# A four-layer graph network on one core: the node stage in three parts per block, five gather passes with single PSUM banks

## The chip, the core and the metric

The kernel runs on one core of a Trainium2 chip. The core has five engines with an instruction queue each: TensorE (PE, with its weight loads as PEld), VectorE (DVE), ScalarE (ACT), GpSimd (POOL) and SyncE (SP, which issues plain DMAs). Each engine works through its own queue in order; engines meet only through semaphores that an instruction waits for or raises. The metric is the device time of one launch in microseconds, median of several runs; lower is better.

## The reference

Inputs are x of 100000 nodes by 128 features, 25000 edges (src, dst, sorted by dst), edge features of 160, edge weights, and the weights of four layers. Everything is float32.

```python
x = layernorm(x + L0(x)); x = layernorm(x + L1(x)); x = layernorm(x + L2(x)); x = layernorm(x + L3(x))
# L0: x + softplus-MLP(segment_sum(edge_attr, dst))
# L1: (x @ Wself.T + mean-like(segment_sum(w * x[src], dst)) @ Wneigh.T + biases) / 2
# L2: relu(x @ w_s + segment_sum((x @ w_n)[src], dst))
# L3: two Chebyshev convolutions, 128 -> 256 (relu) -> 128, each of three terms,
#     lap(h) = segment_sum(w[:, None] * h[src], dst), terms x, lap(x), 2 * lap(lap(x)) - x
```

Only nodes that are the end of an edge differ from the plain per-node chain "add, normalize, multiply, normalize, ...". The kernel uses that: it does the plain chain for all 100000 nodes, and the edges' corrections for 25000 slots.

## The kernel before

The edges are cut into 196 tiles of 128, four tiles to a quad, 49 quads (`QUADS`). Nodes are cut into 196 blocks of 512 (`BLOCKS`). The program is fully unrolled; the order of the instructions is written out by hand in "turns": turn c does the first step of item c, a later step of item c-1, and so on. A `Signal` is a semaphore that counts the turns of one producer; `s.wait(engine, pass, g, back=n)` waits until the producer has done item g-n. Between stages all five engines meet (`enter`, `leave`).

The stages in order are: a setup that builds index tables; `tgt0` and `src0` (edge rows through the first layers); `nodes`; then the gather passes `L1`, `L2`, `T1`, `T2`, `LH`; and `LU`, which scatters the finished rows over the output. The change touches `nodes` and the five passes from L1 to LH; tgt0, src0 and LU keep their order.

**The node stage** (`row_pass("nodes", BLOCKS)`) takes one block per turn. In the names of the profile: GpSimd adds a constant (y0, L599); TensorE turns y0 (L1383) and ScalarE copies it out of PSUM (yTa, L1137); TensorE multiplies it (p1, L1527); VectorE takes the moments of y0 (bn, L969, and mv, L974) and makes y1 from p1 (L1023); TensorE turns y1, ScalarE copies it (yTb), TensorE multiplies (p2, L1533); VectorE makes u2 (L1037) and its moments; GpSimd makes x3 from u2, four instructions (L622), and x3b, which is x3 plus the row gb2 (L609); TensorE turns x3, ScalarE copies it (yTc), TensorE makes h (L1547, two matrix products into two banks), ScalarE its relu (hT, L1273), TensorE p3 (L1540); VectorE adds x3b (y3, L1043), takes the moments; ScalarE makes the square root (sd3, L1142) and, after VectorE's reciprocal (rs3, L991) and offset (off3, L999), the output rows (outb, L1307), which SP stores. GpSimd also issues two small look-ups per block (L647). Turn c does y0, p1 and y1 of block c, p2 and u2 of block c-1, x3 of c-2, h of c-3, p3 and y3 of c-4, and sd3 and the output of c-5.

**A gather pass** (`edge_pass`) takes one quad per turn. GpSimd gathers four times 128 rows (L563); ScalarE scales them with the edge weight (L1154, not in L2); TensorE turns them into `bank(g.b)`, one of two PSUM banks (L1401); VectorE runs the scan along the sorted edges that sums each segment (L853); TensorE multiplies the sums (L1426 to L1485), and VectorE and ScalarE finish the row, which SP stores as the next pass's table. In T2 TensorE makes a first product (L1453), VectorE adds a loaded array (L903), ScalarE takes the relu (L1236), TensorE multiplies it (L1480) and turns it (L1485), and ScalarE copies both out (L1210, L1213). GpSimd gathers quad g after the sums of quad g-3:

```python
run_turns(QUADS, 0, lambda g: gather(p, g, table_, index, rows, g.r, width, rows_in, [(summed, 3)]))
```

A layout's `bank(n)` is PSUM bank n as four pieces of 128 columns; `g.b` alternates between two buffers, `g.r` runs round four.

Of the kernel before, what the change touches and what calls it, by code (L numbers as in the profile page):

```python
# [9 lines left out]
ALU = mybir.AluOpType  # L25
ACT = mybir.ActivationFunctionType

P = 128
# [3 lines left out]
HID = 256  # L32
# [10 lines left out]
RING = 4  # L43
assert TILES == 4 * QUADS and QUADS % 2 == 1 and BLOCKS % 2 == 0

# [64 lines left out]
def gnn_kernel(nc, x, src, dst, attr, ew, W1, b1, W2, b2, Wself, bself, Wneigh, bneigh, ws, wn, G1, gb1, G2, gb2, out):  # L110
    ctx = ExitStack()
    with ctx:
# [54 lines left out]
        xin, y0, y1, u2, x3, x3b, outb = (sb(n, [P, 2, 4, P]) for n in ("xin", "y0", "y1", "u2", "x3", "x3b", "outb"))  # L167
# [10 lines left out]
        lk = sb("lk", [P, 2, 4])  # L178
# [4 lines left out]
        pre_in = (y0, x3b, xin, outb)  # L183
# [9 lines left out]
        SELF, NEIGH = (5, 3), (7, 6)  # L193
        HALVES = ((6, 7), (3, 5))
        FIRST = (5, 7)

# [11 lines left out]
        LATE = {"tgt0": 3, "L1": 1, "L2": 1, "T1": 1, "T2": 1, "LH": 1, "LU": 1}  # L208
# [5 lines left out]
        def transfer(name, at_once=2, **n):  # L214
# [6 lines left out]
        x_in = transfer("x_in", nodes=1)  # L221
        xe_in = transfer("xe_in", RING, L1=1, L2=1, T1=1, LH=1, LU=1)
        pre_arrived = transfer("pre_arrived", RING, T2=1)
# [4 lines left out]
        look_in = transfer("look_in", nodes=2)  # L228
        out_st = transfer("out_st", tgt0=1, src0=1, nodes=1)
        oe_st = transfer("oe_st", RING, L1=1, L2=1, T1=1, T2=1, LH=1)  # L230
        more_st = transfer("more_st", src0=1, T1=1, T2=1, LH=1)
# [5 lines left out]
        x3b_made = signal("x3b_made", "nodes")  # L237
# [3 lines left out]
        y3_made, bn3, mv3, rs3, off3_made, looked_up = (  # L241
            signal(n, "nodes") for n in ("y3_made", "bn3", "mv3", "rs3", "off3_made", "looked_up"))
# [11 lines left out]
        out_made = signal("out_made", "tgt0 nodes L1 L2 LH LU")  # L254
# [4 lines left out]
        sd1, h_kept = signal("sd1", "src0"), signal("h_kept", "src0 T2")  # L259
        sd3 = signal("sd3", "nodes")  # L260
        hidden = signal("hidden", {"nodes": 2, "T2": 1})
# [7 lines left out]
        y0_turned, p1_made, y1_turned, p2_made, x3_turned, h_made = (  # L269
            signal(n, "src0 nodes") for n in ("y0_turned", "p1_made", "y1_turned", "p2_made", "x3_turned", "h_made"))  # L270
# [6 lines left out]
        h_turned = signal("h_turned", "T2")  # L277
# [44 lines left out]
        spb, = (yTc[:, n, :] for n in range(1))  # L322
# [3 lines left out]
        LOADS, EDGE_LOADS = 15, 12  # L326
        COUNTED = [c for c in range(TILES) if c % 3 == 0]
        PUT = [c for c in range(TILES) if c % 3 != 0]
        V_COLS, V_WEIGHTS, V_BTC, V_TABLE = 1, 2, 3, 4
        T_TURNED, T_FOLDED, T_A1, T_COUNTED = 1, 2, 3, 4  # L330
# [5 lines left out]
        def _(sp):  # L336
# [6 lines left out]
            with nc.allow_non_contiguous_dma("edge lists with an edge per partition; columns of biases"):  # L343
# [15 lines left out]
                for t, s in ((b1_col, b1), (bs_col, bself), (bn_col, bneigh)):  # L359
                    load(t[:, :], s.rearrange("(p a) -> p a", a=1))  # L360
# [16 lines left out]

            def edge_pass(p, state=None, store=None):
                def state_load(g):
                    if state is None or not g.inside(QUADS):  # L380
                        return
                    if p in ("L1", "T1"):
                        turned.wait(sp, p, g, back=RING)
                    if p == "L2":
                        step.wait(sp, p, g, back=RING)
                    if p == "LH":
                        out_made.wait(sp, p, g, back=RING)
                    if p == "LU":
                        step.wait(sp, p, g, back=RING, k=2)
                    sp.dma_start(xe[:, g.r], quad_of(state, g)).then_inc(xe_in.of(g), 16)  # L390

                def more_load(g):
                    if not g.inside(QUADS):
                        return
                    if p == "T2":
                        pre_added.wait(sp, p, g, back=RING)
                        sp.dma_start(flat(pre_in[g.r]), one(h_pre, g)).then_inc(pre_arrived.of(g), 16)
                    if p == "LU":
                        step.wait(sp, p, g, back=2, k=3)
                        sp.dma_start(gb_in[:, g.b], quad_of(state3, g)).then_inc(x3_in.of(g), 16)  # L400

                def turn(g):
                    state_load(g.less(-3))
                    more_load(g.less(-3 if p == "T2" else -1))
                    g = g.less(LATE[p])
                    if not g.inside(QUADS):
                        return
                    if p == "T1":
                        lap_kept.wait(sp, p, g)
                    elif p == "T2":  # L410
                        near_kept.wait(sp, p, g)
                    elif p != "LU":
                        out_made.wait(sp, p, g)
                    if store is not None:
                        sp.dma_start(quad_of(store, g), oe[:, g.r]).then_inc(oe_st.of(g), 16)
                    if p == "T1":
                        pre_kept.wait(sp, p, g)
                        sp.dma_start(one(h_pre, g), hb[:, g.b].rearrange("p k d -> p (k d)")).then_inc(more_st.of(g), 16)
                    if p == "T2":
                        h_kept.wait(sp, p, g)  # L420
                        sp.dma_start(quad_of(state_h, g), hb[:, g.b]).then_inc(more_st.of(g), 16)
                    if p == "LH":
                        u_kept.wait(sp, p, g)
                        sp.dma_start(quad_of(lap2, g), y1[:, g.b]).then_inc(more_st.of(g), 16)

                enter(sp, p)
                for c in range(3):
                    state_load(Turn(c))
                for c in range(3 if p == "T2" else 1):
                    more_load(Turn(c))  # L430
                run_turns(QUADS, LATE[p], turn)
                if store is not None:
                    oe_st.wait_all(sp, p)
                if p in more_st.n:
                    more_st.wait_all(sp, p)
                leave(sp)

# [58 lines left out]
            def x_load(g):  # L496
                if g.inside(BLOCKS):
                    y0_made.wait(sp, "nodes", g, back=2)
                    sp.dma_start(xin[:, g.b], block_of(x, g)).then_inc(x_in.of(g), 16)

            def nodes_turn(g):
                x_load(g.less(-2))
                g5 = g.less(5)
                if g5.inside(BLOCKS):
                    out_made.wait(sp, "nodes", g5)
                    if g5.c == BLOCKS - 1:
                        out_st.wait(sp, "nodes", g5, back=1)
                    sp.dma_start(block_of(out, g5), outb[:, g5.b]).then_inc(out_st.of(g5), 16)

            enter(sp, "nodes")  # L510
            x_load(Turn(0))
            x_load(Turn(1))
            run_turns(BLOCKS, 5, nodes_turn)
            out_st.wait_all(sp, "nodes")
            leave(sp)

            edge_pass("L1", state1, store=state2)
            edge_pass("L2", state2, store=state3)
            edge_pass("T1", state3, store=lap1)
            edge_pass("T2", store=near_out)  # L520
            edge_pass("LH", near_out, store=most_out)
            edge_pass("LU", most_out)
# [3 lines left out]
        def _(pool):  # L526
# [64 lines left out]
            def make_y0(p, g):  # L591

                (x_in if p == "nodes" else x_gathered).wait(pool, p, g)
                y0_turned.wait(pool, p, g, back=2)
                bn0.wait(pool, p, g, back=2)
                if p == "src0":
                    x1_most.wait(pool, p, g, back=2)
                    x1_made.wait(pool, p, g, back=2)
                gp.tensor_tensor(y0[:, g.b], xin[:, g.b], all4(c0h[:, :]), ALU.add).then_inc(y0_made.sem, 1)  # L599

            def row_pass(p, n, meanwhile):
                def turn(g):
                    next_, g2, g3 = g.less(-1), g.less(2), g.less(3)
                    if next_.inside(n):
                        make_y0(p, next_)
                    if p == "nodes" and g3.inside(n):
                        x3_made.wait(pool, p, g3)
                        y3_made.wait(pool, p, g3, back=2)
                        gp.tensor_tensor(x3b[:, g3.b], x3[:, g3.b], all4(gb2_row[:, :]), ALU.add).then_inc(x3b_made.sem, 1)  # L609
                    meanwhile(g)  # L610
                    if p == "src0" and g.inside(n):
                        rs0.wait(pool, p, g)
                        out_st.wait(pool, p, g, back=2)
                        gp.tensor_scalar(outb[:, g.b, 3, :], y0[:, g.b, 3, :], mv[:, 0, g.b, 3, 0:1], rs[:, 0, g.b, 3:4],
                                         ALU.subtract, ALU.mult).then_inc(x1_made.sem, 1)
                    if p == "nodes" and g2.inside(n):

                        x3_turned.wait(pool, p, g2, back=2)
                        x3b_made.wait(pool, p, g2, back=2)
# [968 lines left out]
```

## Time and profile before

| | us |
|---|---|
| three timed runs | 4190.33, 4184.45, 4193.7; median 4190.33 |
| span of the profiled execution | 4620.6 |
| node stage in the profiled execution, from 1073 to 2481 | 1408 |
| passes L1, L2, T1, T2, LH in it | 316, 308, 312, 310, 333 |
| LU in it | 561 |

The profiled execution's own time is known only as its span: it lies 430 us above the median of the timed runs, and it is no outlier of those runs. Stage lengths are read from it, from the first DMA that SyncE issues in a stage to the first of the next. An engine's "busy" time counts an instruction that overlaps its neighbour on the same engine only once. In a timeline, consecutive instructions of one line are merged, with their count behind an x; what an instruction costs its queue is therefore read from start to start, and what it costs someone who waits for it from start to end. A matmul of float32 appears as two instructions, a transpose as one, and the ends of matmuls are modelled.

### The profile page before, as it was taken

How to read it: one execution, taken by the hardware profiler on the slowest of the kernel's cores; microseconds unless marked ns; L12 is line 12 of the kernel's file. 1: busy time of each engine (PE TensorE's matmuls, PEld its weight loads, DVE VectorE, ACT ScalarE, POOL GpSimd, SP SyncE). 2: the span in 40 equal slices, each digit the busy share in tenths (PEclk: the TensorE clock that was granted, in tenths of full speed). 3: DMA queues.
4: the chain of work that ended last, by engine and by line, in shares of the span. 5: the costliest groups of instructions: out<-in, count | busy, mean ns of one | idle time of the engine just before them, and what ended most of it. 6: DMA issues, size and time to landing. Idle time of an engine off the chain costs nothing.

```text
span 4620.6 us, 74892 instructions
## 1 busy us (share of the span) xinstructions
PE 3327.5 (72%) x20670; PEld 2626.7 (57%) x20670; DVE 3081.8 (67%) x12829; ACT 2499.0 (54%) x7360; POOL 3172.0 (69%) x3630
## 2 busy tenths in 40 slices
PE   2278977778999999999995665658878878821111
PEld 0135646666888888888884654654446667721111
DVE  2298979997888888888885775761224434554454
ACT  0005768996888888888884552115546633311110
POOL 6506668876888888888885665656656646567676
PEclk6598989998999999999997787878989989955555
DMA  0005645662222222222222443435657756632222
GB/s 21 4 1 173 184 133 182 215 216 97 79 75 79 75 79 75 79 75 79 75 79 77 130 131 107 137 123 195 226 192 267 268 195 211 206 109 89 87 91 70
DMA packets 311878, 575.84 MB, mean 125 GB/s; under 512 B 69502, under 2 KB 97975, under 8 KB 311466
## 3 DMA queue, kind: packets, MB, share of 16 engines
q1 hardware_dynamic: 235178, 443.56, 28.5%
q0 software_dynamic: 76288, 127.51, 10.3%
q8 instruction: 171, 2.80, 0.3%
q14 instruction: 241, 1.97, 0.1%
HBM read 301.23 MB, written 271.14 MB: 124 GB/s over the span
## 4 chain that ended last, share of the span: by engine, by line
DVE 42%; issue 17%; PE 15%; another core or an unknown queue 11%; POOL 7%; ACT 5%; DMA 1%; DVEq 0%; SPq 0%; POOLq 0%; ACTq 0%; PEldq 0%; PEld 0%
DVE bn L969 11%; DVE y L1023 5%; DVE mv L974 4%; PE ps L1444 4%; POOL rows L563 3%; DVE u L1037 3%; DVE y L1043 3%; DVE x L853 2%; POOL out_dram L678 2%; PE ps L1383 2%; DVE bn L861 2%; DVE x3b L853 1%; PE ps L1401 1%; PE ps L1462 1%
## 5 line engine op out<-in xcount | busy, mean ns | idle before, releaser
L563 POOL DMA_INDIRECT rows<-state,rows_of_src x588 | 555.8, 945 | 378.6 <-issue 161.7
L853 DVE TENSOR_TENSOR_SCAN x<-same,x,ps 128x512 f32<-128x512 uint8 x336 | 428.8, 1276 | 303.8 <-remote 176.4
L1401 PE MATMUL ps<-ident,rows 128*128 128x128 f32 x1372 | 288.9, 317 | 438.6 <-ACT rows L1154 239.5
L1137 ACT ACTIVATE yTa<-ps 128x512 f32<-128x512 f32 x392 | 232.9, 594 | 567.7 <-PE ps L1383 295.5
L563 POOL DMA_INDIRECT rows<-lap,rows_of_lap x392 | 383.4, 978 | 210.1 <-issue 110.3
L1401 PEld LDWEIGHTS ps<-ident,rows 128*128 128x128 f32 x1372 | 203.6, 166 | 492.0 <-issue 304.7
L647 POOL DMA_INDIRECT lk<-node_table,look_idx x392 | 388.5, 991 | 91.9 <-issue 82.2
L1154 ACT ACTIVATE rows<-rows,lap_w 128x128 f32<-128x128 f32 (+1 forms) x784 | 269.8, 419 | 287.1 <-DMA rows<-lap,rows_of_lap 232.0
L1142 ACT ACTIVATE sd<-mv,consts 128x4 f32<-128x4 f32 x588 | 174.6, 297 | 438.7 <-DVE mv L865 163.8
L1540 PE MATMUL ps<-V,hT 128*128 128x128 f32 x3136 | 405.1, 283 | 8.4 <-ACT hT L1273 8.4
L969 DVE BATCH_NORM_STATS2 bn<-y 128x6 f32<-128x128 f32 x1764 | 378.7, 276 | 23.2 <-POOL y L599 23.1
L1540 PEld LDWEIGHTS ps<-V,hT 128*128 128x128 f32 x3136 | 367.6, 193 | 45.7 <-ACT hT L1273 42.0
L622 POOL TENSOR_SCALAR x<-u,negm,rs 128x128 f32<-128x128 f32 x784 | 339.5, 441 | 72.5 <-issue 61.3
L1547 PE MATMUL ps<-yTc,G 128*128 128x512 f32 x784 | 369.3, 593 | 1.9 <-ACT yTc L1137 1.9
L599 POOL TENSOR_TENSOR y<-xin,c0h 128x512 f32<-128x512 f32 x245 | 311.1, 1270 | 38.3 <-DMA xin<-in_x_dram 28.6
L1307 ACT ACTIVATE outb<-y,off,rs 128x128 f32<-128x128 f32 x784 | 322.5, 491 | 6.6 <-DVE off L999 6.6
L1383 PE MATMUL ps<-ident,x 128*128 128x128 f32 x1372 | 233.2, 298 | 124.3 <-DVE y L949 115.6
L1383 PEld LDWEIGHTS ps<-ident,y 128*128 128x128 f32 x1960 | 232.6, 143 | 148.8 <-issue 131.3
L1527 PE MATMUL ps<-A,yTa 128*128 128x128 f32 x1960 | 283.4, 288 | 34.2 <-ACT yTa L1137 24.1
L1286 ACT ACTIVATE unused<-y 128x128 bf16<-128x128 f32 x980 | 289.6, 310 | 0.0
L1383 PE MATMUL ps<-ident,y 128*128 128x128 f32 x1960 | 260.0, 276 | 38.8 <-POOL y L599 36.3
L1023 DVE SCALAR_TENSOR_TENSOR y<-ps,rs,b1c 128x128 f32<-128x128 f32 x980 | 276.0, 344 | 13.8 <-issue 2.6
(269 smaller groups left out, 9346.5 us busy)
## 6 DMA issues: line engine op xcount, KB each, us to landing
state_h<-hb SPq DMA_DIRECT2D x98, 512.0 KB
xin<-in_x_dram SPq DMA_DIRECT2D x196, 256.0 KB
out_dram<-outb SPq DMA_DIRECT2D x196, 256.0 KB
xe<-state SPq DMA_DIRECT2D x147, 256.0 KB
state<-outb SPq DMA_DIRECT2D x98, 256.0 KB
state<-oe SPq DMA_DIRECT2D x98, 256.0 KB
h_pre<-hb SPq DMA_DIRECT2D x49, 512.0 KB
rows<-in_edge_attr_10x_dram SPq DMA_DIRECT2D x48, 320.0 KB
```

Source lines behind the costliest of these rows:

```text
L563: gp.indirect_dma_start(out=dest[:, at, k, 0:width], out_offset=None, in_=table_, in_offset=bass.IndirectOffsetOnAxis(ap=index[:, c:c + 1] ...
L599: gp.tensor_tensor(y0[:, g.b], xin[:, g.b], all4(c0h[:, :]), ALU.add).then_inc(y0_made.sem, 1)
L622: i = gp.tensor_scalar(x3[:, g2.b, k, :], u2[:, g2.b, k, :], negm[:, g2.b, k:k + 1], rs[:, 2, g2.b, k:k + 1], ALU.add, ALU.mult)
L647: gp.indirect_dma_start(out=lk[:, g.b, 2 * j:2 * j + 2], out_offset=None, in_=node_table, in_offset=bass.IndirectOffsetOnAxis(ap=look_idx[ ...
L853: v.tensor_tensor_scan(t[0:np_, g.b].rearrange("p k d -> p (k d)"), same[0:np_, 512 * g.c:512 * g.c + 512], ps[0:np_, bk + g.b, :], t[0:np ...
L969: i = v.bn_stats(bn[:, n, k, :], y[:, k, :])
L1023: i = v.scalar_tensor_tensor(y1[:, g.b, k, :], bank(3)[:, k, :], dev(0, g.b, k), b1c[:, :], ALU.mult, ALU.add)
L1307: i = a.activation(outb[:, g5.b, k, :], y3[:, g5.b, k, :], ACT.Identity, bias=off3[:, g5.b, k:k + 1], scale=rs[:, 3, g5.b, k:k + 1])
L1383: i = t.transpose(bank(bk)[:, k, :], source[:, k, :], ident[:, :])
L1401: i = t.transpose(bank(g.b)[:, k, :], rows[:, g.r, k, 0:P], ident[:, :])
L1540: i = t.matmul(bank(7)[:, k, :], hT[:, j, k, :], V02[:, j, :], start=j == 0, stop=j == 1)
L1547: i = t.matmul(ps[:, 5 + j, :], G02[:, j * P:(j + 1) * P], yTc[:].rearrange("p k d -> p (k d)"), start=True, stop=True)
```

## The change

**Node stage.** A turn becomes three parts (`node_part(q)`, with q // 3 the block), and each engine's queue lists the steps of the same block closer together: the last step, the output, is now four blocks late instead of five, y3 two and not four. VectorE makes x3 in one step with gb2 added, from u2, the reciprocal root and the row gb2; GpSimd's x3 and x3b are gone. What x3 lacks (the subtracted mean) and has too much (gb2) is folded into the next weights in the setup (`G02c`, `gb1c_col`: one more load, three more products, four more small vector instructions). The two look-ups write straight into `looked`, and VectorE's copy and the negated mean are gone. x is loaded three blocks ahead into four buffers, not two. The index rows (`index_rows`, `index_weights`) come behind the stage's last turn and no longer among its last turns. The names `shared`, `SHARE` and `PLAN` provide for node parts inside the passes; all shares are zero, so every block stays in this stage.

**Passes L1 to LH** (`merged_pass`). The rows' transposes go to one bank (`SUMS`), the products to two (`LEFT`, `RIGHT`), all other transposes to one (`TURNED`). TensorE takes the sums of quad g and the product of quad g-1 in turn g, VectorE and ScalarE finish quads g-1 to g-3. GpSimd gathers three quads ahead, and quad g after the sums of quad g-4. LU stays as it was.

```diff
-                            i = gp.tensor_scalar(x3[:, g2.b, k, :], u2[:, g2.b, k, :], negm[:, g2.b, k:k + 1],
-                                                 rs[:, 2, g2.b, k:k + 1], ALU.add, ALU.mult)
-                        gp.tensor_tensor(x3b[:, g3.b], x3[:, g3.b], all4(gb2_row[:, :]), ALU.add).then_inc(x3b_made.sem, 1)
...
+            def node_part(q):
+                p, n = "nodes", BLOCKS
+                g, part = Turn(q // PARTS), q % PARTS
+                g1, g2, g3 = (g.less(k) for k in (1, 2, 3))
...
+                if part == 1:
...
+                    if g3.inside(n):
+                        y3_made.wait(dve, p, g3)
+                        stats(2, y3[:, g3.b], bn3)
+                        bn3.wait(dve, p, g3)
+                        aggregate(2, g3.b, mv3)
+                if part == 2:
...
+                    if g3.inside(n):
+                        sd3.wait(dve, p, g3)
+                        final_made.wait(dve, p, g3, back=2)
+                        v.reciprocal(rs[:, 3, g3.b, :], sd[:, 3, g3.b, :]).then_inc(rs3.sem, 1)
+                    if g1.inside(n):
+                        rs2.wait(dve, p, g1)
+                        x3_turned.wait(dve, p, g1, back=2)
+                        for k in range(4):
+                            i = v.scalar_tensor_tensor(x3[:, g1.b, k, :], u2[:, g1.b, k, :], dev(2, g1.b, k), gb2_row[:, :],
+                                                       ALU.mult, ALU.add)
+                        i.then_inc(x3_made.sem, 1)
...
+                    if g2.inside(n):
+                        p3_made.wait(dve, p, g2)
+                        x3_made.wait(dve, p, g2)
+                        final_made.wait(dve, p, g2, back=2)
+                        v.tensor_tensor(y3[:, g2.b], bank(4 if shared else 7), x3[:, g2.b], ALU.add).then_inc(y3_made.sem, 1)
...
+                    if g3.inside(n):
+                        root(p, g3, sd3, mv3, sd[:, 3, g3.b, :], mv[:, 2, g3.b, :, 1], EPS1)
+                if part == 2:
+                    if g4.inside(n):
+                        off3_made.wait(act, p, g4)
+                        out_st.wait(act, p, g4, back=2)
+                        for k in range(4):
+                            i = a.activation(outb[:, g4.b, k, :], y3[:, g4.b, k, :], ACT.Identity,
+                                             bias=off3[:, g4.b, k:k + 1], scale=rs[:, 3, g4.b, k:k + 1])
+                        i.then_inc(final_made.sem, 1)
+                    if g.inside(n):
+                        keep(p, g, y1T_kept, y1_turned, [(p2_made, 1)], yTb[:, :, :], 0 if shared else 1)
...
+                def rows_of(g):
+                    if g.inside(QUADS):
+                        gather(p, g, table_, index, rows, g.r, width, rows_in, [(summed, RING)])
...
+                    for k in range(4):
+                        i = t.transpose(bank(SUMS)[:, k, :], rows[:, g.r, k, 0:P], ident[:, :])
...
+                    if p == "T1" and g1.inside(QUADS):
+                        before_relu(g1)
+                        keep(p, g1, lap_kept, lap_turned, [], oe[:, g1.r], TURNED)
...
+                    if p == "T1" and g.c > 1:
+                        lap_kept.wait(pe, p, g, back=2)
```

The instructions' order on three engines shows what moved. A row is a line, an operation, what it writes and reads, its shape, and the semaphores it waits for.

VectorE in the middle of the node stage, before: from the moments of y3 (bn3, mv3) of one block to the reciprocal of its root.

```order
L969 BN_STATS bn<-y 128x6 [waits y3_made]
L969 BN_STATS bn<-y 128x6 x3
L974 BN_AGGR mv<-bn 128x2 [waits bn2]
L974 BN_AGGR mv<-bn 128x2 x3
L974 BN_AGGR mv<-bn 128x2 [waits bn3]
L974 BN_AGGR mv<-bn 128x2 x3
L1058 TENSOR_SCALAR negm<-mv 128x4 [waits mv2]
L1061 SCALAR_TENSOR_TENSOR tmpv<-ssum,mv 128x4 [waits squared]
L969 BN_STATS bn<-y 128x6 [waits y0_made]
L969 BN_STATS bn<-y 128x6 x3
L991 RECIPROCAL rs<-sd 128x4 [waits out_made,sd3]
L974 BN_AGGR mv<-bn 128x2 [waits bn0]
```

VectorE at the same place in the change, from y1 of block g (L1116) over the moments of y3 of block g-3 to y3 of block g-2.

```order
L1116 SCALAR_TENSOR_TENSOR y<-ps,rs,b1c 128x128 [waits y1_turned,squared,p1_made,rs0]
L1116 SCALAR_TENSOR_TENSOR y<-ps,rs,b1c 128x128 x3
L1011 BN_STATS bn<-y 128x6 [waits y3_made]
L1011 BN_STATS bn<-y 128x6 x3
L1016 BN_AGGR mv<-bn 128x2 [waits bn3]
L1016 BN_AGGR mv<-bn 128x2 x3
L1127 RECIPROCAL rs<-sd 128x4 [waits sd2]
L1131 RECIPROCAL rs<-sd 128x4 [waits final_made,sd3]
L1136 SCALAR_TENSOR_TENSOR x<-u,rs,gb_row 128x128 [waits x3_turned,rs2]
L1136 SCALAR_TENSOR_TENSOR x<-u,rs,gb_row 128x128 x3
L1141 SCALAR_TENSOR_TENSOR off<-mv,rs 128x4 [waits rs3]
L1147 TENSOR_TENSOR y<-ps,x 128x512 [waits final_made,x3_made,p3_made]
```

Behind mv3 stood four rows that need nothing from sd3; now one reciprocal stands there, and x3 and y3 behind it. y3 waits for `final_made`, ScalarE's output rows of block g-4 in the same turn, since the two share a buffer.

ScalarE in the middle of the node stage, before, one turn:

```order
L1137 ACTIVATE yTa<-ps 128x512 [waits p1_made,y0_turned]
L1142 ACTIVATE sd<-mv,consts 128x4 [waits mv3]
L1137 ACTIVATE yTb<-ps 128x512 [waits p2_made,y1_turned]
L1273 ACTIVATE hT<-ps,gb_col 128x512 [waits p3_made,h_made]
L1273 ACTIVATE hT<-ps,gb_col 128x512
L1142 ACTIVATE sd<-tmpv,consts 128x4 [waits tv2]
L1142 ACTIVATE sd<-mv,consts 128x4 [waits mv0]
L1137 ACTIVATE yTc<-ps 128x512 [waits h_made,x3_turned]
L1286 ACTIVATE unused,ssum<-y 128x128 [waits squared,tv2,y1_made]
L1286 ACTIVATE unused,ssum<-y 128x128 x3
L1307 ACTIVATE outb<-y,off,rs 128x128 [waits out_st_1,off3_made]
L1307 ACTIVATE outb<-y,off,rs 128x128 x3
```

ScalarE in the change, one turn:

```order
L1307 ACTIVATE yTa<-ps 128x512 [waits p1_made,y0_turned]
L1307 ACTIVATE yTc<-ps 128x512 [waits h_made,x3_turned]
L1461 ACTIVATE unused,ssum<-y 128x128 [waits squared,tv2,y1_made]
L1461 ACTIVATE unused,ssum<-y 128x128 x3
L1312 ACTIVATE sd<-mv,consts 128x4 [waits mv0]
L1312 ACTIVATE sd<-tmpv,consts 128x4 [waits tv2]
L1489 ACTIVATE hT<-ps,gb1c_col 128x512 [waits h_made,p3_made]
L1489 ACTIVATE hT<-ps,gb1c_col 128x512 [waits h_made]
L1312 ACTIVATE sd<-mv,consts 128x4 [waits mv3]
L1498 ACTIVATE outb<-y,off,rs 128x128 [waits out_st_1,off3_made]
L1498 ACTIVATE outb<-y,off,rs 128x128 x3
L1307 ACTIVATE yTb<-ps 128x512 [waits p2_made,y1_turned]
```

The root that waits for mv3 stood second in a turn and stands now directly ahead of the output rows; the copy yTb, which TensorE's p2 waits for, stood ahead of hT and now stands behind the output rows, last in the turn.

TensorE in pass T2, before, one turn (sums of the next quad, first product, second product and transposes of the previous quad):

```order
L1401 MATMUL ps<-ident,rows 128x128 [waits carried,weighed]
L1401 MATMUL ps<-ident,rows 128x128 x3
L1453 MATMUL ps<-x,G2x 128x512 [waits pre_added,carried]
L1453 MATMUL ps<-x,G2x 128x512
L1480 MATMUL ps<-V,u 128x128 [waits near_kept,hidden]
L1480 MATMUL ps<-V,u 128x128 x7
L1485 MATMUL ps<-ident,u 128x128 [waits h_kept]
L1485 MATMUL ps<-ident,u 128x128 x7
```

TensorE in pass T2 in the change, one turn:

```order
L1953 MATMUL ps<-ident,hTm 128x128 [waits near_kept,unfolded]
L1953 MATMUL ps<-ident,hTm 128x128 x3
L1932 MATMUL ps<-agg,G2x 128x512 [waits pre_added,carried]
L1932 MATMUL ps<-agg,G2x 128x512
L1953 MATMUL ps<-ident,hTm 128x128 [waits h_kept]
L1953 MATMUL ps<-ident,hTm 128x128 x3
L1890 MATMUL ps<-ident,rows 128x128 [waits carried,weighed]
L1890 MATMUL ps<-ident,rows 128x128 x3
L1961 MATMUL ps<-V,hTm 128x128 [waits h_kept]
L1961 MATMUL ps<-V,hTm 128x128 x7
```

The eight transposes of the hidden rows (L1485) had two banks and one wait; now they are two groups of four (L1953) in the bank that the second product (L1961) also uses, each behind a copy of ScalarE's.

## Rows read from the trace of the kernel before

**Rows 1.** The page: first line, and the chain that ended last.
```profile
span 4620.6 us, 74892 instructions
...
DVE 42%; issue 17%; PE 15%; another core or an unknown queue 11%; POOL 7%; ACT 5%; DMA 1%; DVEq 0%; SPq 0%; POOLq 0%; ACTq 0%; PEldq 0%; PEld 0%
```

**Rows 2.** Windows by stage: length; busy PE, PEld, DVE, ACT, POOL; clock, DMA, GB/s.
```profile
701.00:1073.00 372.00, 273.91 (x1704) 228.39 (x1704) 338.88 (x1464) 339.46 (x1103) 270.19 (x272) 0.97 0.57 205
...
1073.00:2481.00 1408.00, 1380.15 (x9408) 1133.40 (x9408) 1219.89 (x7272) 1193.63 (x3921) 1214.41 (x1568) 0.99 0.25 75
...
2481.00:2797.00 316.00, 192.75 (x1176) 179.48 (x1176) 215.75 (x735) 161.87 (x488) 184.94 (x196) 0.78 0.40 122
...
2797.00:3105.00 308.00, 187.17 (x1176) 174.47 (x1176) 213.00 (x731) 43.83 (x101) 185.96 (x196) 0.79 0.41 126
...
3105.00:3417.00 312.00, 251.75 (x980) 139.74 (x980) 63.91 (x54) 167.73 (x392) 184.88 (x196) 0.93 0.63 207
...
3417.00:3727.00 310.00, 255.42 (x1568) 196.79 (x1568) 118.21 (x98) 179.25 (x343) 184.91 (x196) 0.94 0.72 248
...
3727.00:4060.00 333.00, 255.99 (x1960) 242.94 (x1960) 152.20 (x147) 108.08 (x246) 188.93 (x200) 0.88 0.63 199
```

**Rows 3.** Chain of waits inside one node turn: start, length, what.
```profile
1506.28 0.78 DVE bn L969 x4
...
1507.14 0.34 DVE mv L974 x4
...
1507.52 0.80 issue
...
1509.85 0.60 DVE u L1037
```

**Rows 4.** Timeline of one node turn: start, length, instructions, [idle before].
```profile
1506.17 0.30 ACT L1142 ACTIVATE sd<-mv,consts 128x4 f32<-128x4 f32 x1 [0.17 <-DVE mv L974]
...
1506.37 0.58 ACT L1137 ACTIVATE yTb<-ps 128x512 f32<-128x512 f32 x1
...
1507.05 1.11 PE L1533 MATMUL ps<-ws_sb,yTb 128*128 128x128 f32 x8
...
1508.16 2.05 PE L1540 MATMUL ps<-V,hT 128*128 128x128 f32 x16
...
1508.51 0.18 DVE L1014 RECIPROCAL rs<-sd 128x4 f32<-128x4 f32 x1
...
1508.72 1.13 DVE L1023 SCALAR_TENSOR_TENSOR y<-ps,rs,b1c 128x128 f32<-128x128 f32 x4
...
1510.01 1.65 ACT L1307 ACTIVATE outb<-y,off,rs 128x128 f32<-128x128 f32 x4
...
1510.05 1.88 PE L1547 MATMUL ps<-yTc,G 128*128 128x512 f32 x4
...
1510.41 1.27 POOL L599 TENSOR_TENSOR y<-xin,c0h 128x512 f32<-128x512 f32 x1
...
1511.77 1.04 PE L1383 MATMUL ps<-ident,y 128*128 128x128 f32 x8
```

**Rows 5.** Timeline, end of the node stage: one instruction of the index rows.
```profile
2464.92 0.36 DVE L1089 TENSOR_TENSOR rows_of_lap<-xe,rows_of_lap 128x196 int32<-128x196 f32 x1
```

**Rows 6.** Timeline in pass L1: GpSimd's gathers, one after a wait.
```profile
2608.00 0.94 POOL L563 DMA_INDIRECT rows<-state,rows_of_src  x1 [0.30 <-issue]
...
2613.37 0.94 POOL L563 DMA_INDIRECT rows<-state,rows_of_src  x1 [4.42 <-PE ps L1401]
```

**Rows 7.** Windows: 100 us inside pass L1.
```profile
2600.00:2700.00 100.00, 62.90 (x403) 58.99 (x404) 73.21 (x253) 54.29 (x165) 62.83 (x68) 0.83 0.42 128
```

**Rows 8.** Timelines of passes T1 and T2: ScalarE instructions.
```profile
3239.31 1.25 ACT L1205 ACTIVATE hb<-ps,gb_col 128x512 f32<-128x512 f32 x2
...
3583.39 1.27 ACT L1154 ACTIVATE rows<-rows,lap_w 128x128 f32<-128x128 f32 x4
...
3600.43 1.06 ACT L1236 ACTIVATE u<-u 128x1024 f32<-128x1024 f32 x1 [0.88 <-issue]
```

More of the change, by code:

```diff
@@ L376, in _ @@
             leave(sp)
[L378 to L436, printed above, removed]
@@ L497, in x_load @@
                 if g.inside(BLOCKS):
[L498 to L508, printed above, removed]
+                    y0_made.wait(sp, "nodes", g, back=RING)
@@ L985, in turn, with node_part @@
+            enter(dve, "src0")
+            run_turns(QUADS, 5, src0_turn)
+            leave(dve)
+            def node_part(q):
+                p, n = "nodes", BLOCKS
+                g, part = Turn(q // PARTS), q % PARTS
+                g1, g2, g3 = (g.less(k) for k in (1, 2, 3))
+                shared = q >= PARTS * ALONE
+                if part == 0:
+                    if g.inside(n):
                         y0_made.wait(dve, p, g)
                         stats(0, y0[:, g.b], bn0)
[L987 to L991 removed]
@@ L1116, in _ @@
+            for p in MERGED:
+                merged_pass(p)
+            edge_pass("LU")
         @block.scalar
@@ L1523, in turn @@
-                    if g.inside(n):
-                        y0T_kept.wait(pe, p, g)
-                        y1_made.wait(pe, p, g, back=1)
-                        for k in range(4):
-                            i = t.matmul(bank(3)[:, k, :], yTa[:, k, :], A1[:, :], start=True, stop=True)
-                        i.then_inc(p1_made.sem, 1)
+                    if not shared:
+                        third_turned()
                     if g1.inside(n):
@@ L1531, in turn @@
                         u2_made.wait(pe, p, g1, back=1)
-                        for k in range(4):
-                            i = t.matmul(bank(4)[:, k, :], yTb[:, k, :], ws_sb[:, :], start=True, stop=True)
-                        i.then_inc(p2_made.sem, 1)
-                    if nodes and g4.inside(n):
-                        hidden.wait(pe, p, g4)
-                        y3_made.wait(pe, p, g4, back=1)
+                        if shared and g3.inside(n):
+                            y3_made.wait(pe, p, g3)
@@ new lines, in node_part @@
+                        products(p2_made, g1, 4, yTb, ws_sb)
+                    if shared:
+                        third_turned()
+                if part == 1:
+                    if g.inside(n):
+                        y0T_kept.wait(pe, p, g)
+                        if not shared:
+                            y1_made.wait(pe, p, g, back=1)
+                        elif g1.inside(n):
+                            u2_made.wait(pe, p, g1)
+                        products(p1_made, g, 4 if shared else 3, yTa, A1)
+                    if g2.inside(n):
+                        x3T_kept.wait(pe, p, g2)
+                        hidden.wait(pe, p, g2, back=1)
+                        for j in range(2):
+                            t.matmul(ps[:, 5 + j, :], G02c[:, j * P:(j + 1) * P], yTc[:].rearrange("p k d -> p (k d)"),
+                                     start=True, stop=True).then_inc(h_made.sem, 1)
```

972 lines of the change are left out of this document (689 added, 283 removed).

## Prediction

> **What bounds the kernel now.** I read the windows by stage first, since a change in one stage is worth what that stage's own bound allows. The node stage lasts 1408 us, and TensorE is busy 1380.15 us of it at a granted clock of 0.99 [rows 2]: 196 blocks of 7.04 us of TensorE work. The timeline of one turn says the same from close by: h starts at 1510.05 and the next block's first transpose at 1511.77, directly behind it [rows 4]. Successive turns lie 7.0 us apart. TensorE sets the pace there. VectorE stands first in the chain that ended last, with 42% of it [rows 1], but in the node stage that chain contains a wait of 0.80 us inside one turn [rows 3], so VectorE has room: it is busy 1219.89 of 1408 us, 6.22 a turn [rows 2].
>
> In the passes no engine is near full. L1 lasts 316 us with TensorE busy for 193 and VectorE for 216 [rows 2]. GpSimd issues a gather every 0.94 + 0.30 = 1.24 us where nothing holds it, so four cost 5.0 us, but it waits up to 4.42 us for TensorE's sums [rows 6]; 68 gathers in 100 us [rows 7] are 17 quads, 5.88 us each. A pass is 49 x 5.88 = 288 us and 28 us of start and end.
>
> **The node turn after the change.** What it takes away lies off the path: GpSimd's x3 and x3b, in a stage where GpSimd is busy 1214 of 1408 us [rows 2] and leads no wait in [rows 3]; two small VectorE instructions. What it adds is x3 on VectorE, four 128x128 instructions. The trace has no such instruction with both tensors in SBUF; the nearest row from below is u2, 0.60 us for 512 columns in one instruction [rows 3], from above GpSimd's y0, 1.27 [rows 4]. I take y1's 1.13 [rows 4], which has the same form and the same four pieces.
>
> What decides is the order. In before, each step of a turn belongs to another block, and an engine that waits finds its input a turn old. In the changed order one ring closes within one turn. Follow it from TensorE's p2 of block g: VectorE's u2, mv0, bn2, mv2, tmpv, the reciprocal, y1 of the next block, then bn3 and mv3 of an older one; ScalarE's sd3 waits for that mv3; behind sd3 in ScalarE's queue stand the output rows, behind these yTb, and p2 of the next block waits for yTb. Every link is either a queue's order or a wait that the orders above name. The price of each link, with 0.04 to 0.10 for a hand-over (0.08 lies between bn's end and mv's start in [rows 3], 0.10 between yTb's end and p2's start in [rows 4]):
>
> sd3 0.05 and 0.20 (start of sd to start of yTb, [rows 4]); output rows 1.65; yTb 0.58; p2 0.10 + 1.11 (all [rows 4]); u2 0.05 + 0.60 [rows 3]; mv0 0.34, bn2 0.78, mv2 0.34 + 0.10 [rows 3]; tmpv 0.15, my estimate from the 0.18 of a reciprocal of the same size [rows 4]; reciprocal 0.21 (start of rs at 1508.51 to start of y1 at 1508.72) and y1 1.13 [rows 4]; bn3 0.78, mv3 0.34 + 0.10 [rows 3]. The sum is 8.61 us. I take 8.6 a turn.
>
> Nothing else in the turn is longer. TensorE needs 7.04. VectorE's own queue, added from the same rows, is three bn (2.34), three mv (1.02), u2 and y3 (1.20), y1 and x3 (2.26) and about 0.75 of small ones, 7.57. x3 and y3 stand behind mv3 on VectorE, beside the output rows and yTb on ScalarE and p2 on TensorE; from sd3's end to u2 there are 3.4 us, and rs3, x3, off3, y3 (0.60) and bn0 (0.78) need about 2.8, so x3 costs nothing up to some 0.65 more than I price it. That takes 8.6 - 7.0 = 1.6 us a turn: 196 x 1.6 = 314 us. The index rows behind the last turn are some 18 instructions in a row on VectorE at 0.36 [rows 5], with the root between them about 8 us, which the last turns hid before. Nodes: +322.
>
> The look-ups, x three blocks ahead and the setup's additions I cost at nothing: x arrives before y0 needs it now (no wait for it in [rows 3]), and the setup's products are single instructions beside hundreds of others; if both were wrong I see no more than 3 us. The tails of the turns (four late, not five) give back at most one turn, 8 us; left out.
>
> A rule that speaks against x3 on VectorE: the Trainium skill ("SBUF — State Buffer", section "Who interferes with whom") says that VectorE and GpSimd share one pair of ports, held by one of them alone, so that a VectorE instruction with two SBUF inputs and a GpSimd instruction exclude each other. By it x3 could stand still while y0 runs; no row of before shows it. By the rows alone x3 is hidden; what the other case gives is rival four.
>
> **The passes.** GpSimd now gathers quad g after the sums of g-4, and those sums come a turn ahead of the product, so I expect the wait of 4.42 [rows 6] to go where no ring is longer. L1 and L2: 49 x 5.0 + 28 = 273, which is -43 and -35. LH: TensorE is busy 256 / 49 = 5.2 a quad [rows 2], so 283, -50.
>
> T1 has a ring through single banks: first product (four 512-column products, twice h's 1.72 from start to start [rows 4], 3.44), a hand-over, two instructions of hb (1.25, [rows 8]), the copy of the turned sums (0.58 as yTb), then two groups of four transposes (half of 1.04 each [rows 4], less their overlap 0.44) and hand-overs: about 6.4. 49 x 6.4 + 28 = 342, +30. T2 has one through the bank of the hidden rows and ScalarE's queue: half the transposes 0.55, copy 0.59, the scaling of four rows that stands next on ScalarE (1.27, [rows 8]), the second copy 0.58, the second product 2.05 (as p3, [rows 4]), the copy 0.59, the relu of the next quad 1.06 [rows 8], and five hand-overs: about 7.2. 381, +71. Together the passes give -43 - 35 + 30 + 71 - 50 = -27.
>
> **Sum.** +322 - 27 = +295. The profiled execution has a span of 4620.6 us, 430 above the median of 4190; no wait that I see in the node stage or the passes belongs to that excess, so I add the difference as it stands: 4190 + 295 = 4485, and a profiled span of about 4916.
>
> **Bounds.** All five passes at 5.0 to 5.2 a quad give 1375 us against 1579, -204: 4190 + 322 - 204 = 4308. L1, L2 and LH as before with T1 and T2 at their rings give +101: 4613.
>
> **The rivals.**
> First: the ring is shorter than I add, and VectorE alone sets the turn at 7.6. For it: hand-overs and the output rows may overlap more than their ends show. 196 x 0.6 = 118, with +8 and -27: 4289. Chance 0.08.
>
> Second, the other side: ScalarE's wait for sd3 doesn't bite, VectorE packs its instructions as closely as in its busy time (6.22 + 1.13 - 0.2 = 7.15), and TensorE keeps 7.0. Then the stage costs +8 and the passes -27: 4171. It decides at a turn of about 7.1, since (27 - 8) / 196 = 0.10. Against it: the ring would have to lose 1.5 us of named links. Chance 0.08.
>
> Third: TensorE, idle for 1.6 us of each 8.6, is granted its lower clock level, 1.2 GHz, and p2 takes 2.2: 196 x 1.1 = 216 more, 4700. For it: L1 with TensorE busy for 61% has a clock of 0.78. Against it: src0 with 273.91 / 372 = 74% has 0.97 [rows 2], and 7.04 / 8.6 is 82%. Chance 0.06.
>
> Fourth: x3 and y0 exclude each other, and x3 is longer by y0's 1.27, of which 0.65 has room: 196 x 0.62 = 122, 4607. Against it: y0 is released by bn0, which lies behind x3 on VectorE, about a turn's quarter away. Chance 0.05.
>
> **The numbers.** My forecast has 0.73. A measurement of this kernel can tell about 0.2% from no change. Faster needs the second rival or nearly all of the passes' best case with a turn under 8: 0.09. Within 0.2%: 0.01. Slower: 0.90. The range takes in the first rival, the bounds of the passes and the fourth: 4280 to 4615.
>
> **What would show it.** The node stage in the profile after should last about 1730 us with turns of 8.6; VectorE should wait for ScalarE (sd3, then the output rows ahead of y3) and for p2 ahead of u2; ScalarE should wait for mv3 with the output rows and yTb behind it; the granted clock should stay above 0.95. In L1, L2 and LH the gathers should follow each other at 1.24 us with no wait for sums; T1 should last about 342 and T2 about 381. I am wrong if TensorE is still busy for 95% of the node stage, if its clock there falls under 0.9, or if T2 ends near 280.

## The result and the profile after

The changed kernel takes 4664.61 us, median of four runs (4659.76 to 4665.31), against 4190.05 before: a ratio of 1.1137, 95% interval 1.1121 to 1.1153. That is 474.6 us slower. The forecast was slower by 295, with a range up to 4615.

The span of its profiled execution is 4662.7 us, so this time the profile and the timed runs agree, which they did not for the kernel before. The windows by stage of the changed kernel (stretch, length; busy PE, PEld, DVE, ACT, POOL; clock, DMA, GB/s) answer to [rows 2]:

```profile
0.00:206.00 206.00, 127.62 (x684) 62.32 (x684) 185.89 (x660) 4.50 (x8) 132.82 (x153) 0.99 0.08 18
...
925.00:2596.00 1671.00, 1417.54 (x9408) 1088.39 (x9408) 1472.69 (x7664) 1215.21 (x3921) 622.87 (x589) 0.99 0.20 63
2596.00:2864.00 268.00, 165.04 (x1176) 153.45 (x1176) 208.36 (x735) 152.91 (x490) 184.74 (x196) 0.88 0.47 145
2864.00:3123.00 259.00, 173.39 (x1176) 158.72 (x1176) 200.16 (x735) 38.49 (x98) 185.85 (x196) 0.86 0.49 150
3123.00:3461.00 338.00, 247.76 (x980) 138.32 (x980) 62.66 (x49) 172.03 (x392) 184.84 (x196) 0.96 0.57 191
3461.00:3866.00 405.00, 270.92 (x1568) 190.38 (x1568) 120.42 (x98) 188.68 (x392) 184.82 (x196) 0.97 0.58 191
3866.00:4134.00 268.00, 233.76 (x1960) 224.16 (x1960) 153.86 (x147) 109.64 (x245) 185.29 (x196) 0.95 0.75 241
4134.00:4663.00 529.00, 96.99 (x392) 76.49 (x392) 279.83 (x833) 72.29 (x245) 403.93 (x392) 0.50 0.31 95
```

The first row is the setup; tgt0 and src0 are left out; then stand the node stage (1671 us), L1, L2, T1, T2, LH and LU. TensorE's share of the node stage fell from 98% to 85%, at a clock of 0.99. The forecast for these stages was 1730, 273, 273, 342, 381 and 283, in all 3282; they took 3209. Against the first profile of before, though, the node stage lost only 262 (1670.1 against 1407.8 from first DMA to first DMA) and the passes gained 36, which gives nothing like 474. (In [rows 2] the passes end at 4060, but SyncE issues LU's first DMA at 4055.5: they took 1575 us and LU 565, not 1579 and 561.) The setup, which was 352 us in that execution, is 206 here, and LU 529.

The chain of waits inside one turn of the changed node stage (start, length, what) is the ring of the forecast:

```profile
1808.26 1.17 PE ps L1776 x8
1809.46 0.69 DVE u L1092
1810.15 0.28 DVE mv L1016 x4
1810.43 0.77 DVE bn L1011 x4
...
1811.92 1.13 DVE y L1116 x4
1813.05 0.79 DVE bn L1011 x4
...
1814.28 0.02 ACT sd L1312
...
1814.48 0.08 ACT outb L1498
...
1814.86 1.25 ACT outb L1498 x3
1816.11 0.49 ACT yTb L1307
...
1816.65 1.17 PE ps L1776 x8
```

From one p2 to the next, 1808.26 to 1816.65, are 8.39 us. Every piece is a link that the forecast named, in its order: p2, u2, mv0, bn2, y1, bn3, and on ScalarE sd3, the output rows and yTb. x3 and y3 don't appear. A turn is 8.39 us on average over the stage, where it was 7.00. GpSimd's y0 and VectorE's x3 run at the same time in no turn of this stage, so the rule of rival four can't be tried on it; x3 took 1.13 us, the value taken.

### The profile page after: what moved, and what is told of

Its sections match the earlier page's. It is cut to its first block, busy times and chain, and to the rows that moved or that the text cites. A ratio compares the mean times of both kernels' runs of the same rounds, so it can differ in the third digit from the quotient of the medians.

```text
span 4662.7 us, 74040 instructions
## 1 busy us (share of the span) xinstructions
PE 3298.3 (71%) x20676; PEld 2520.4 (54%) x20676; DVE 3315.5 (71%) x13225; ACT 2519.9 (54%) x7409; POOL 2586.4 (55%) x2650
## 4 chain that ended last, share of the span: by engine, by line
DVE 28%; POOL 24%; PE 16%; issue 13%; ACT 13%; DMA 5%; SPq 0%; POOLq 0%; ACTq 0%; DVEq 0%
POOL rows L599 15%; DVE bn L1011 7%; ACT outb L1498 5%; PE ps L1776 5%; DVE y L1116 5%; DVE mv L1016 4%; POOL out_dram L713 4%; PE ps L1926 4%; DMA state_h<-hb 3%; DVE u L1092 3%; POOL node_put L587 3%; ACT yTb L1307 2%; POOL xin L599 2%; PE ps L1961 1%; ACT hb L1536 1%
## 5 line engine op out<-in xcount | busy, mean ns | idle before, releaser
L1193 DVE TENSOR_TENSOR_SCAN agg<-same,agg,ps 128x512 f32<-128x512 uint8 x240 | 304.9, 1271 | 299.1 <-PE ps L1890 288.2
L665 POOL DMA_INDIRECT looked<-node_table,look_idx x392 | 372.9, 951 | 91.8 <-issue 67.3
L1669 PE MATMUL ps<-ident,rows 128*128 128x128 f32 x392 | 103.7, 361 | 423.2 <-ACT rows L1324 409.6
L1854 PE MATMUL ps<-yTc,G02c 128*128 128x512 f32 x784 | 369.0, 593 | 0.7 <-ACT yTc L1307 0.7
L1669 PEld LDWEIGHTS ps<-ident,rows 128*128 128x128 f32 x392 | 64.7, 184 | 443.5 <-ACT rows L1324 415.2
L1521 ACT ACTIVATE rows<-rows,lap_w 128x128 f32<-128x128 f32 (+1 forms) x588 | 207.7, 425 | 175.9 <-DMA rows<-state_h,rows_of_src 130.7
L1776 PE MATMUL ps<-ws_sb,yTb 128*128 128x128 f32 x1960 | 282.7, 288 | 21.6 <-ACT yTb L1307 0.8
L1324 ACT ACTIVATE rows<-rows,lap_w 128x128 f32<-128x128 f32 x196 | 62.6, 389 | 425.8 <-DMA rows<-lap,rows_of_lap 425.8
L1776 PEld LDWEIGHTS ps<-ws_sb,yTb 128*128 128x128 f32 x1960 | 241.5, 194 | 67.7 <-ACT yTb L1307 67.7
L1016 DVE BATCH_NORM_AGGREGATE mv<-bn 128x2 f32<-128x6 f32 x2744 | 258.0, 156 | 16.9
```

Of the source, the lines that this page charges most:

```text
L665: gp.indirect_dma_start(out=looked[:, c, 2 * j:2 * j + 2], out_offset=None, in_=node_table, in_offset=bass.IndirectOffsetOnAxis(ap=look_id ...
L1016: i = v.bn_aggr(mv[:, n, b, k, :], bn[:, n, k, :])
L1193: v.tensor_tensor_scan(t[:, g.b].rearrange("p k d -> p (k d)"), same[:, 512 * g.c:512 * g.c + 512], ps[:, bk, :], t[:, 1 - g.b, 3, P - 1:P ...
L1776: i = t.matmul(bank(bk)[:, k, :], lhs[:, k, :], w[:, :], start=True, stop=True)
L1854: t.matmul(ps[:, 5 + j, :], G02c[:, j * P:(j + 1) * P], yTc[:].rearrange("p k d -> p (k d)"), start=True, stop=True).then_inc(h_made.sem, 1)
```

## The experiments

**The kernel before, profiled again.** No edit.

> The kernel before, unchanged, profiled a second time. Theory: the 430 us by which its profiled execution was longer than its median are waits of one execution that the chain can put down to nothing (523 us of them in the chain: setup 124, L2 79, T2 70, LH 95, LU 131), so an execution without them has a span near 4188, a setup near 206 us like that of the changed kernel, and passes of some 270 to 290 us each. Rival: the excess belongs to every profiled execution of this kernel; then the span is near 4620 again with the same stages.

It took 4185.29 us, with a span of 4183.5: no excess. Its windows by stage (same columns):

```profile
0.00:206.00 206.00, 127.19 (x678) 62.27 (x678) 184.41 (x656) 4.24 (x8) 132.89 (x151) 0.98 0.08 18
...
920.00:2328.00 1408.00, 1379.89 (x9408) 1133.61 (x9408) 1219.54 (x7272) 1193.51 (x3921) 1214.58 (x1568) 0.99 0.25 75
2328.00:2599.00 271.00, 171.21 (x1176) 160.15 (x1176) 214.95 (x735) 160.81 (x490) 185.00 (x196) 0.85 0.47 143
2599.00:2862.00 263.00, 166.33 (x1176) 148.02 (x1176) 212.52 (x735) 42.32 (x98) 185.85 (x196) 0.90 0.49 148
2862.00:3125.00 263.00, 239.42 (x980) 138.49 (x980) 62.66 (x49) 168.63 (x392) 184.93 (x196) 0.95 0.75 245
3125.00:3392.00 267.00, 244.07 (x1568) 189.97 (x1568) 118.25 (x98) 177.80 (x343) 184.98 (x196) 0.97 0.85 290
3392.00:3655.00 263.00, 230.94 (x1960) 221.90 (x1960) 153.90 (x147) 110.33 (x245) 185.68 (x197) 0.97 0.78 246
3655.00:4184.00 529.00, 96.78 (x392) 76.63 (x392) 279.70 (x833) 72.30 (x245) 404.08 (x392) 0.50 0.31 95
```

The node stage is the same 1408 as in [rows 2]. The five passes take 1327 and not 1575. The two profiled executions lie 437 us apart: 248 of them in the passes, 146 in the setup, 36 in LU and 7 in tgt0 and src0. In this profile the passes run at GpSimd's pace all along. One of its gathers in L1 (timeline, idle before in brackets); those beside it have the same 0.30, and the 4.42 of [rows 6] has no counterpart: GpSimd's waits for TensorE's sums come to 2.2 us in the whole of L1, where the first profile has 35.0.

```profile
2400.50 0.94 POOL L563 DMA_INDIRECT rows<-state,rows_of_src  x1 [0.30 <-issue]
```

In the first profile the excess was to be seen. Its setup, in the chain of waits, holds pieces like this one; the chain names nothing that caused them:

```profile
91.15 15.14 another core or an unknown queue
```

**The node stage of before in the changed kernel.** All five engines get the old turns back; the setup and the passes stay as changed.

```diff
-            for q in range(PARTS * ALONE):
-                node_part(q)
...
+            old_pass("nodes", BLOCKS)
```

> The changed kernel with the node stage of before. Theory: the two parts of the change add; the node stage gives back its 262 us, 4665 - 262 = 4403, and what is left over 4190, some 213 us, is the passes, whose gain in the profiles was taken against disturbed passes of before. Rival: the node stage is the whole loss of 474 and the passes are even: 4190.

4394.17 us (1.0492 of before, 1.0475 to 1.0510): 270 under the changed kernel, and 204 over before. The first reading holds: the passes cost 204 in the timed runs, and the node stage 270. That the two make up the whole loss follows from taking one kernel between the other two; the profiles say the same independently. In this kernel's profile the node stage lasts 1406 us and the five passes 1535, against 1408 and 1327 in the second profile of before, and the setup 206 in both.

**yTb ahead of the output rows.**

```diff
-y3 = sb("y3", [P, 2, 4, P])
+y3 = sb("y3", [P, RING, 4, P])
...
                 if part == 2:
+                    if g.inside(n):
+                        keep(p, g, y1T_kept, y1_turned, [(p2_made, 1)], yTb[:, :, :], 0 if shared else 1)
                     if g4.inside(n):
...
-                    if g.inside(n):
-                        keep(p, g, y1T_kept, y1_turned, [(p2_made, 1)], yTb[:, :, :], 0 if shared else 1)
```

> The changed kernel with ScalarE's copy yTb ahead of the output rows and y3 in four buffers, so that y3 does not wait for them. Theory of the ring: it loses the output rows' 1.6 us, the next bound is VectorE's 7.5 us a turn, so 196 x 0.87 = 170 us less, near 4495. Rival, VectorE itself sets 8.4 a turn: no change, 4665.

4586.58 us: 78 less, under half of what was expected. The output rows were on the ring, but a second ring stood close behind it. The chain of one turn, u2 to u2:

```profile
1808.50 0.69 DVE u L1092
...
1810.97 1.14 DVE y L1116 x4
...
1812.15 0.66 PE ps L1651 x4
1812.80 1.79 PE ps L1873 x16
1814.59 0.99 PE ps L1651 x8
1815.58 0.91 PE ps L1776 x8
1816.51 0.69 DVE u L1092
```

Behind y1 now stand TensorE's transposes of y1, p3, two more groups of transposes and p2, in TensorE's own queue: 8.01 us from u2 to u2.

**Half of p3 left out**, on top of that edit (the second half of the hidden columns isn't added).

```diff
-                            for j in range(2):
+                            for j in range(1):
```

> The kernel with yTb ahead of the output rows, with half of p3's products left out (the second half of the hidden columns is not added). There a second ring sets 8.0 us a turn: TensorE's y1 transposes, p3 (1.79), two more groups of transposes and p2, then VectorE's u2 to y1. Theory: without half of p3 the ring is 7.1 and VectorE's busy 7.5 a turn takes over: 196 x 0.5 = 100 us under that kernel's 4587, near 4487. Rival: VectorE sets 8.0 itself, no change.

4586.47 us, no change; a turn takes 8.02 us on average in both kernels. So the second ring wasn't alone either. The chain of a turn:

```profile
1803.25 0.29 DVE mv L1016 x3
1803.57 0.31 ACT sd L1312
...
1804.50 0.62 DVE x L1136 x2
1805.17 0.66 PE ps L1651 x4
1805.83 0.91 PE ps L1776 x8
1806.76 0.69 DVE u L1092
...
1814.77 0.69 DVE u L1092
```

A third ring, 8.01 us from u2 to u2, runs from mv3 through sd3, the reciprocal, x3 (which stands behind that reciprocal on VectorE) and its transposes to the same p2. The rival's "no change" came true, but by this chain VectorE's work alone doesn't set the 8.0: the ring leaves VectorE for sd3, the transposes and p2. That is read from the chain; no run cuts the third ring.

**Half of x3 left out** (two of its four pieces aren't computed).

```diff
-                        for k in range(4):
+                        for k in range(2):
                             i = v.scalar_tensor_tensor(x3[:, g1.b, k, :], u2[:, g1.b, k, :], dev(2, g1.b, k), gb2_row[:, :],
```

> The changed kernel with two of x3's four pieces on VectorE left out (half of x3 is not computed). Theory of the ring: x3 lies beside the output rows and costs nothing, so 4665 within 15 us. Rival, VectorE's own work sets the turn: 0.56 x 196 = 110 us less, near 4555.

4659.82 us, 5 less, and the turn stays at 8.39. In the changed kernel x3 is hidden.

**T2's stores ahead of the load.**

```diff
-                    state_load(g.less(-early))
+                    if p != "T2":
+                        state_load(g.less(-early))
...
                         oe_store(g3, near_kept)
+                    if p == "T2":
+                        state_load(g.less(-early))
```

> The changed kernel with one edit in pass T2: SyncE issues the load of h_pre behind the two stores of the turn, not ahead of them. The theory after the profile: T2's longer ring runs through SyncE's queue, where the store of state_h (5.4 us to landing) waits behind a load that waits for VectorE, 15.45 us for two turns. Without it the single-bank ring is left that the prediction put at 7.2 a turn: T2 falls from 405 to about 381, the whole to about 4641. Rival: the banks' ring alone sets 405; no change.

The chain in T2 of the changed kernel, on which that expectation rests (its ring holds two quads, 15.47 us from one of its copies oe to the next):

```profile
3602.25 0.60 ACT oe L1563
3602.85 0.95 ACT hTm L1566
...
3603.85 0.66 PE ps L1953 x4
3604.51 1.73 PE ps L1932 x4
...
3606.26 1.24 DVE hTm L1251
...
3607.51 0.32 SPq L486
...
3607.88 5.43 DMA state_h<-hb
...
3613.33 0.60 ACT hb L1543
...
3617.72 0.60 ACT oe L1563
```

VectorE's sum frees the buffer for the load of h_pre; in SyncE's queue the store of state_h waits behind that load, and the copy hb, which writes to the buffer that is stored, waits for the store. With the stores first the kernel took 4636.51 us, 28 less, and T2 380 us between its first loads and LH's: what the forecast had put it at.

**Banks of their own in T2**, with the stores first. ScalarE also takes the relu of the next quad ahead of the copy that waits for the second product.

```diff
-                        product.wait(act, p, g2)
...
+                    if p == "T2" and g2.inside(QUADS):
+                        product.wait(act, p, g2)
...
-                        near_kept.wait(pe, p, g, back=1)
...
+                    h_kept.wait(pe, p, g, back=1, k=half + 1)
...
-                            i = t.transpose(ps[:, TURNED, (2 * (k % 2) + j) * P:(2 * (k % 2) + j + 1) * P],
+                            i = t.transpose(ps[:, 4 + half, (2 * (k % 2) + j) * P:(2 * (k % 2) + j + 1) * P],
...
-                            i = t.matmul(bank(TURNED)[:, k, :], hTm[g.b][:, j, k, :], V02[:, j, :], start=j == 0, stop=j == 1)
+                            i = t.matmul(bank(6)[:, k, :], hTm[g.b][:, j, k, :], V02[:, j, :], start=j == 0, stop=j == 1)
```

> As the kernel with the stores first, and in T2 the two halves of the hidden rows' transposes have banks 4 and 5 and the second product bank 6 for themselves, and ScalarE takes the relu of the next quad ahead of the copy that waits for the second product. Theory: the ring through the bank of the hidden rows is what T2 costs; T2 falls to TensorE's 5.2 a quad, 265 to 283, the whole to 4525 to 4545. Rival: TensorE, taking the steps of two quads in turn, or GpSimd's gathers stay late; T2 stays above 340.

4540.25 us, 124 under the changed kernel; T2 282 us. How much of the 98 us under the last kernel's T2 the banks give and how much the relu's place, no run separates. What is left over the 267 of before goes, by the chain, with a ring over the gathers: a DMA of 6.00 us to landing, scaling, relu, transposes, sums, and the next gathers.

**A bank of its own in T1.**

```diff
-                        turn4(p, g1, lap_turned, agg[:, g1.b], TURNED)
+                        turn4(p, g1, lap_turned, agg[:, g1.b], 6)
...
-                keep(p, g1, lap_kept, lap_turned, [], oe[:, g1.r], TURNED)
+                keep(p, g1, lap_kept, lap_turned, [], oe[:, g1.r], 6)
```

> The changed kernel with one edit in pass T1: the transposes of the summed rows have bank 6 for themselves and no longer share one with the state's. Theory: the ring of 6.45 us (first product 3.45, hb 1.27, copy 0.6, transposes 0.63 and 0.44) opens at the copy; what is left is first product and hb, 4.8, under the gathers' 5.0: T1 falls from 338 to about 265 to 275, the whole by 63 to 73, near 4595. Rival: ScalarE or the stores set T1; it stays above 320.

4602.65 us, 62 less; T1 275 us. The chain in T1 of the changed kernel was, for one quad:

```profile
3305.49 3.45 PE ps L1926 x8
...
3308.96 0.46 ACT hb L1536
...
3309.54 0.68 ACT hb L1536
3310.22 0.50 ACT oe L1307
...
3310.86 0.63 PE ps L1651 x4
3311.48 0.44 PE ps L1890 x4
3311.92 3.45 PE ps L1926 x8
```

6.43 us, link for link the 6.4 of the forecast. In the edited kernel only the first product (3.69) and hb are left, 5.12.

**The node stage of before with these passes.** The edits of T1 and T2 on the kernel with the old node stage.

> The node stage of before, and the changed passes with both edits of T1 and T2 (own banks, stores first, relu ahead). Theory, the parts add: 4394 - 62 (T1) - 124 (T2) = 4208, 0.4% over before. Rival: the passes share something (a queue, TensorE's clock), and the sum misses by more than 15 us.

4211.30 us (1.0058, 1.0043 to 1.0072). The parts add, within 3 us.

**T1's and T2's last rings.** On top of the last kernel: T1's first product in two pairs of banks in turn; in T2 and LH ScalarE scales a quad one turn ahead of its sums.

```diff
-                                i = t.matmul(ps[:, LEFT + j, :], w[:, j * P:(j + 1) * P], r.rearrange("p k d -> p (k d)"),
+                                i = t.matmul(ps[:, LEFT + 2 * g.b + j, :], w[:, j * P:(j + 1) * P], r.rearrange("p k d -> p (k d)"),
...
-                    weigh(g.less(-2))
+                    weigh(g.less(-1 if p in ("T2", "LH") else -2))
```

> As that kernel, with T1's first product in two pairs of banks in turn, and in T2 and LH ScalarE scales a quad one turn ahead of its sums and not two, so that its wait for the gathered rows does not stand ahead of the steps that free the rows' buffers. Theory: T1's ring of 5.12 us (first product 3.69, hb 1.27) and T2's ring over gathers, scaling, relu and sums (11.3 us for two quads) open, and all five passes go at GpSimd's 4 x 1.25 us: 260 to 266 each, 1310 in all against before's 1327, so 4165 to 4180, 0.2 to 0.6% under before. Rival: scaling one turn ahead comes too late for the sums, and T2 and LH are longer than 283 and 268: 4205 or more.

4179.93 us, 0.998 of before (0.9972 to 0.9989): the one version under before, by a fifth of a per cent. Its windows for L1 to LH give 267, 259, 264, 270 and 263, in all 1323 where before has 1327. Inside the passes nothing more is to be had while GpSimd issues four gathers of 1.25 us for each quad: it waits for TensorE's sums about 1 us in all five. What is left stands at the seams: GpSimd waits five times for SyncE at the start of a pass, 101 us together.

## Why the prediction was wrong

**The node stage: right mechanism, 52 us too much.** The ring was there, with the links that were named. It is 8.39 and not 8.61: bn, with 0.77 to 0.79, and y1, 1.13, came out as taken, while the hand-overs behind mv and between yTb and p2 were shorter (0.04 where 0.10 was taken, between yTb and p2), and yTb stands 0.49 on the path, not 0.58. u2 was taken too low, 0.60 for 0.69, since the chain of [rows 3] cuts it off where the next instruction starts. The turn grew by 1.39 and not 1.6: 196 x 1.39 = 272, not 314. The index rows cost the 8 us that were estimated. The run-out, left out of the forecast, gave 13 back: without the index rows 40 us lie between the last y0's start and the stage's end, where 53 did. In the profiles the stage lost 262, by exchange of the stage alone 270, where 322 was forecast. The first rival (VectorE alone, at 7.6) fell: the turn is 8.39, and with the first ring cut two others of 8.0 stood there. The second rival fell: ScalarE's wait for sd3 is on the chain in nearly every turn (176 of 179 between 1000 and 2500 us). The third fell too: TensorE's granted clock stayed at 0.99 with TensorE busy for 85%. The fourth wasn't put to the test, since x3 and y0 don't meet.

**The passes after: right in sum, in part by luck.** 1552 forecast, 1538 measured, with T2 over its forecast by 24 and the other four under theirs by 38. T1 came at 338 for 342. T2 came at 405 for 381: the ring of 7.2 was there, but a longer one lay over it through SyncE's queue, which the forecast didn't walk; with that queue's order mended T2 took 380. LH's 283 rests on TensorE being busy for 256 us at a granted clock of 0.88 [rows 2]; in the second profile of before it is 231 at 0.97. And the mechanism of L1, L2 and LH was wrong: the change took no wait for sums away there, since the undisturbed kernel had hardly any (4.7 us in all five passes). Against the second profile of before these three changed by -3, -4 and +5 us, where -43, -35 and -50 were forecast; T1 and T2 changed by +75 and +138, for +30 and +71.

**What failed is the sum.** The forecast said of the 430 us by which the profiled execution exceeded the median: "no wait that I see in the node stage or the passes belongs to that excess, so I add the difference as it stands". It did belong there. 248 us of the excess lay in the five passes, and the wait of 4.42 in [rows 6], which was read as a bound of the kernel, was a part of it. In the second profile, whose run took 4185.29 us like the timed ones, the passes of before are 1327, not 1579, so the term of -27 should have read 1552 - 1327 = +225. The exchange measured +204. With the node stage's 322 the corrected sum would have been 547 and 4737, over the 4664.61 that was measured: the passes' term was 231 too low, the node stage's 52 too high, and the two misses pulled against each other. The upper bound of 4615 failed for the same reason: it counted L1, L2 and LH "as before" and T1 and T2 against the lengths of that one execution.

[rows 1] had the sign of it: "another core or an unknown queue 11%" of 4620 is 508 us, and no wait of that name stood in the node stage. Taken stage by stage the chain would have put 79 of them in L2, 70 in T2 and 95 in LH, which makes those passes about 230, 240 and 238 before other bounds step in. (It would not have given the sizes: L1 and T1 have 12 each under that name and were each 47 longer than in the second profile, and LU has 131 and was 36 longer.) GpSimd's 4 x 1.25 x 49 = 245 was the bound that the timed runs had, and it could be read from [rows 6].

What held the engines in that one execution stays open: its records name no cause, and none of the eleven profiles taken since shows it.

## What to carry to other kernels

When a profiled execution is longer than the timed runs, find the stages in which the difference lies before any row of them is taken as a bound: the shares of waits that no record explains, stage by stage, hint at some of them (here not at L1 and T1), and another profile of the same kernel settles it. A pass that looks as if it had slack may have none. In a software pipeline written out by hand, add up each ring that closes within one turn, through every queue it touches, the DMA issuing one too; cutting the longest ring is worth only the distance to the next, which here was 0.4 of 8.4 us and not the 0.9 to the busiest engine.

## What the runs showed that was not expected

One execution of an unchanged program had 146 us more in its setup, 248 in the gather passes and 36 in the last pass than another, while the node stage took 1408 us in both and tgt0 and src0 agreed within 8: it was disturbed in some stages and not at all in others.

The store of 512 KB from hb took 5.43 us on the path behind a load that it didn't depend on, and moving it ahead in SyncE's queue gave 25 us in 49 quads.
